# The first block turned tile by tile, block 1's root on ScalarE, and block 1 turned earlier

## What is computed

```python
xn = _layernorm(x, axis=-1)
# branch 1
h = tanh(einsum('btd,ed->bte', xn, W1) + b1)
s = (einsum('btd,od->bto', h, w2) + b2)[..., 0]
e = exp(s - max(s))
ctx = cumsum(e * xn) / cumsum(e)              # along the sequence
attn = tanh(concat(ctx, xn) @ Wc.T + bc)
# branch 2, integer weights scaled by 1/127
ffn = (silu(xn @ wg.T) * (xn @ wu.T)) @ wd.T  # hidden width 768
out = x + attn + ffn
```

## Time and profile before

| what | us |
|---|---|
| median of 3 runs | 393.87 (393.25 to 393.88) |
| the profiled execution | 393.06 |
| its span, first to last instruction | 391.1 |
| TensorE (PE) busy in it | 385.9 |
| VectorE (DVE) busy | 297.5 |
| ScalarE (ACT) busy | 235.6 |
| GpSimd (POOL) busy | 210.1 |

### The profile page before, as it was taken

One profiled execution on the slowest core, in us unless ns is written; L12 is line 12 of the kernel. 1 busy time (PEld: TensorE's weight loads), 2 busy tenths in 40 slices (PEclk: granted clock), 3 DMA queues, 4 the chain that ended last, 5 costly groups with the idle time before them and its releaser, 6 DMA issues.

```text
span 391.1 us, 7885 instructions
## 1 busy us (share of the span) xinstructions
PE 385.9 (99%) x2740; PEld 268.7 (69%) x2740; DVE 297.5 (76%) x632; ACT 235.6 (60%) x434; POOL 210.1 (54%) x289
## 2 busy tenths in 40 slices
PE   8999999999999999999999999999999999999996
PEld 4556676757566686866877676767677676676765
DVE  6799998999996997876769966777676765754351
ACT  4766576689985659786556575364553644536250
POOL 1487586874629989794335405866456554502000
PEclk9999999999999999999999999999999999999999
DMA  8944525576834232475210005043231220100001
GB/s 275 348 158 69 137 53 134 106 189 89 201 72 96 54 83 81 116 165 97 76 34 29 27 28 164 28 128 87 58 72 55 90 85 26 54 28 28 28 28 61
DMA packets 54945, 36.56 MB, mean 93 GB/s; under 512 B 31858, under 2 KB 50292, under 8 KB 54900
## 3 DMA queue, kind: packets, MB, share of 16 engines
q1 hardware_dynamic: 54608, 35.73, 35.5%
q10 hardware_dynamic: 292, 0.26, 0.2%
HBM read 20.19 MB, written 8.45 MB: 73 GB/s over the span
## 4 chain that ended last, share of the span: by engine, by line
PE 97%; DVE 2%; issue 0%; DVEq 0%
PE bank L707 44%; PE bank L743 41%; PE bank L763 9%; PE bank L1381 1%; DVE ex L1121 0%; DVE stats L951 0%; PE bank L700 0%; PE bank L1377 0%; DVE veps L980 0%; DVE xt L1091 0%; DVE bank L1116 0%; DVE sg L1413 0%; PE bank L813 0%; DVE mv L955 0%; PE bank L819 0%
## 5 line engine op out<-in xcount | busy, mean ns | idle before, releaser
L743 PE MATMUL bank<-xt,narrow 128*128 128x512 f16 x768 | 177.3, 379 | 0.0
L743 PEld LDWEIGHTS bank<-xt,narrow 128*128 128x128 f16 x768 | 75.2, 98 | 75.4 <-DVE wide L1121 0.2
L707 PE MATMUL bank<-narrow,wide 128*128 128x256 f16 x792 | 96.4, 273 | 0.0
L707 PE MATMUL bank<-narrow,xt 128*128 128x256 f16 x768 | 92.8, 273 | 0.3 <-DVE xt L1091 0.3
L707 PEld LDWEIGHTS bank<-narrow,xt 128*128 128x128 f16 x768 | 75.0, 98 | 19.0 <-DVE xt L1091 0.6
L1258 POOL TENSOR_TENSOR wide<-ex,wide 128x512 f16<-128x512 f32 x32 | 39.4, 1248 | 87.6 <-ACT wide L909 87.6
L888 ACT ACTIVATE sg<-bank 128x512 f32<-128x512 f32 x96 | 57.2, 596 | 46.3 <-PE bank L743 45.6
L1116 DVE SCALAR_TENSOR_TENSOR bank<-bank,sg 128x512 f32<-128x512 f32 x96 | 66.1, 694 | 24.4 <-PE bank L743 21.3
L707 PEld LDWEIGHTS bank<-narrow,wide 128*128 128x128 f16 x792 | 77.5, 98 | 9.4
L895 ACT ACTIVATE wide<-bank 128x512 f16<-128x512 f32 x90 | 53.3, 596 | 47.7 <-DVE bank L1116 39.3
L1121 DVE TENSOR_TENSOR wide<-bank,wide 128x512 f16<-128x512 f32 x90 | 60.5, 678 | 9.9 <-ACT wide L895 8.6
(11 more groups left out here) (103 smaller groups left out, 262.3 us busy)
## 6 DMA issues: line engine op xcount, KB each, us to landing
rows<-scratch SPq DMA_DIRECT2D x16, 512.0 KB, 5.1
out_y<-xres SPq DMA_DIRECT2D x31, 256.0 KB, 2.1
xres<-in_x SPq DMA_DIRECT2D x15, 512.0 KB, 5.1
xt<-xt SPq DMA_TRANSPOSE x56, 2.5
wide<-in_wg SPq DMA_DIRECT2D x1, 768.0 KB, 5.9
wide<-in_wu SPq DMA_DIRECT2D x1, 768.0 KB, 8.4
wide<-in_wd SPq DMA_DIRECT2D x1, 768.0 KB, 10.1
wide<-in_wc SPq DMA_DIRECT2D x1, 512.0 KB, 11.1
```

Of the source, the lines that this page charges most:

```text
L707: return pe.matmul(dst, lhs, rhs, start=False, stop=stop, skip_group_check=True)
L743: mm = pe.matmul(b[:, :], pg.up(which, k, j), pg.xn(sx, k, tok), start=n == 0, stop=n == len(todo) - 1)
```

## The change

- The first block is turned tile by tile: `turn_tile` (step L0) turns one tile of 128 tokens into its own bank, X0 (ScalarE) and Y0 (VectorE) make its high part and remainder, and `first_scores` takes the tiles as they come: high parts with W1's high part for all four tiles, then with W1's remainder, then the remainders. Normalising signals after each tile.
- The bias of block 0's S isn't seeded by ScalarE: four float32 products of one row (`seed_first`), two for each of the two banks, stand behind the warm-ups, which are 6 and not 12; one pair of fills follows instead of two. Ea and the spreading of b1 and w2 on TensorE go. b1 and w2 come by two broadcasting DMAs on SyncE's queue, b1 between wu and wd, w2 between x of block 2 and wc; ScalarE's Ss waits for the first and VectorE's first Sv for the second.
- ScalarE takes the square root straight from the variance, with eps as the bias; VectorE's step that adds eps is gone. Block 1's root is made in this way too (step Rq, then R by `root_first`), without GpSimd's Newton rounds. The silu table (Tb) is loaded behind it.
- GpSimd converts wg and wu in halves of three groups each. Its normalising keeps x * r + s; its cost in `STEP` is 1.1 instead of 0.75.
- Block 1's turns are placed at 2.0 instead of 2.5. Th of blocks 0 and 1 writes to SBUF (`rows`) and frees its bank; their Sv is due 25 us after S instead of 0.8.

```diff
-    "T": (PO, 1.35, 1.45), "N": (PO, 3.2, 3.3), "Cl": (PO, 1.2, 1.3), "Lp": (PO, 0.75, 0.85), "Xm": (PO, 1.5, 1.6),
+    "T": (PO, 1.35, 1.45), "N": (PO, 3.2, 3.3), "Cl": (PO, 1.2, 1.3), "Lp": (PO, 1.1, 1.2), "Xm": (PO, 1.5, 1.6),
...
-BEGIN = {TE: 7.3, SE: 5.7, VE: 8.1, PO: 1.0, SY: 12.0}
-SENT = {"W1h": 6.0, "Ea": 7.0, "Wgh": 9.4, "Wuh": 12.8,
+BEGIN = {TE: 6.9, SE: 5.7, VE: 7.8, PO: 1.0, SY: 12.0}
+SENT = {"W1h": 6.4, "Wgh": 8.9, "Wuh": 12.5,
         "Wdh": 22.0, "K1": 36.0, "Kc": 38.0, "Wch": 50.0}
-X_SENT = (0.0, 11.1, 20.0)
+X_SENT = (0.0, 10.4, 20.0)
...
-        turn = 2.5 + 3.55 * (i - 1) if i else -2
+        turn = (2.0 if i == 1 else 2.5 + 3.55 * (i - 1)) if i else -2
...
-            due["Th", i, pr], due["Sv", i, pr] = end["S", i, pr] + 0.1, end["S", i, pr] + 0.8
+            due["Th", i, pr], due["Sv", i, pr] = end["S", i, pr] + 0.1, end["S", i, pr] + (25.0 if i < AWAY else 0.8)
...
     if kind == "Tb":
-        return [(("Xh", 0, 1), 0)]
+        return [(("X0", 0, 3), 0), *((("Rq", g, 0), 0) for g in range(1, ROOTS))]
+    if kind == "Rq":
+        return [(("B", i, 1), 0)]
...
+        def turn_tile(pe, t):
+            pe.wait_ge(v_xn, t + 1)
+            for k in range(KD):
+                mm = pe.transpose(bank_of(fits, "L0", 0, t)[:, k * P:(k + 1) * P], xnat[:, t // 2, t % 2, k * P:(k + 1) * P], ident[:, :])
+            mm.then_inc(p_x0, 1)
+
+        def first_scores(pe, pr):
...
+            if not pr:
+                pe.wait_ge(a_w, 1)
+                for t in range(4):
+                    pe.wait_ge(a_x0, t + 1)
+                    onto(t, 0, 0)
+                pe.wait_ge(v_w, 1)
+                for t in range(4):
+                    onto(t, 0, 1)
+            for t in (2 * pr, 2 * pr + 1):
+                pe.wait_ge(v_x0, t + 1)
+                mm = onto(t, 1, 0, True)
+            mm.then_inc(p_s, 1)
...
+        def square_root(act, g):
+            act.wait_ge(v_mv, 2 * g + 2)
+            act.activation(rstd[:, columns(g)], mv[:, columns(g), 1], ACT.Sqrt, bias=eps[:, 0:1]).then_inc(a_root, 1)
...
             elif kind == "Ss":
-                act.wait_ge(a_b, 1)
                 act.wait_ge(p_warm, 1)
+                act.wait_ge(s_b1, 16)
...
-                act.activation(b[:, :], b[:, :], ACT.Tanh, scale=1.0 / pg.sum_up).then_inc(a_s, 1)
+                act.activation(rows[:, i, n, :] if i < AWAY else b[:, :], b[:, :], ACT.Tanh, scale=1.0 / pg.sum_up).then_inc(a_s, 1)
...
             elif kind == "Sv":
                 if (i, n) == (0, 0):
-                    dve.wait_ge(a_b, 1)
+                    dve.wait_ge(s_w2, 16)
...
             sp.dma_start(half(wu32.bitcast(I32)), rows_of(wu)).then_inc(s_wu, 16)
+            sp.dma_start(b1_every, biases[0:D].partition_broadcast(P)).then_inc(s_b1, 16)
             sp.dma_start(wd32.bitcast(I32).rearrange("p (k n) -> p k n", k=KH), rows_of(wd)).then_inc(s_wd, 16)
             load_x(sp, 2)
+            sp.dma_start(w2b, w2b2_in[0:D].partition_broadcast(P)).then_inc(s_w2, 16)
...
-            to_every(bank[BANKS - 1], 0, b_row)
-            to_every(bank[BANKS - 1], D, w2_row).then_inc(p_b, 1)
...
-            for n in range(FILL):
-                warm_up(spare_bank)
+            for n in range(2):
+                seed_first(n)
+
+            for n in range(WARM, WARM + FILL):
+                warm_up(n)
```

## The result

The changed kernel takes 395.99 us in the median of 11 runs (394.35 to 397.4), the kernel before 393.39 us beside it (11 runs, 392.99 to 394.2). The ratio is 1.006, with a 95% interval of 1.0042 to 1.0077: slower by 1.7 to 3.0 us, where 393.5 was forecast with a range up to 395.1. The runs also spread more, over 3.05 us against 1.2. The profiled execution took 395.93 us with a span of 394.1 (before: 391.1).

The account below looks back on a forecast made before the run. PE's back-to-back matmuls were taken as the bound. First S 0.7 earlier, less a 0.9 stall before S(1,0), put the milestone at 26.1 against 26.46: 0.35 gained, so 393.5 us against a median of 393.87, range 392.5 to 395.1.

Parts of the forecast that it names:

- The opening: From warm-ups to PE's first S: first S at 8.56 instead of 9.26, 0.7 us earlier.
- from 5.34 on 0.265: Opening's bias seeds on PE: a record takes 0.53 at half clock, 0.265 from 5.34 us on.
- The third rival: Opening: clock not up in time, seeds, fills and transposes at half clock; +4.5 us, 398; chance 0.05.
- The w2b wait: VectorE: Sv, set ahead of H 0, waits for w2b landing at 16.5; H 0 at 18.05, now 16.35.
- The stall of 0.9: PE before S(1,0): waits for its bias seed, starting at 20.0 against 19.14.
- Block 1: Block 1's statistics, root and normalising: small steps to 13.5, Lp 14 to 16.2, no new wait.
- The silu table: ScalarE's table load behind block 1's root: load 1.28, Sg 0 at 15.0 to 15.6, cost nothing.
- Block 2: VectorE's root for block 2 ends near 26.85, GpSimd's rounds 3.0 us later; no cost taken.
- the second rival: PE near 40 us waits for block 2's last transpose: net +0.9, 394.8, slower; chance 0.15.
- The rest of the span: PE after the milestone: the same matmuls, back to back, so no change in time.
- It does less than it says: Rival: a second small wait behind Hh 0, 0.3 to 0.8; 393.9 to 394.3, no change; chance 0.15.

Follow-up runs that it names:

- e10: Changed kernel with only the planner's cost of Lp (GpSimd's normalising) put back to 0.75 and 0.85: 395.16 us, ratio 1.0047.
- e14: Kernel before with tanh of blocks 0 and 1 in SBUF and wu's conversion started with the first dot product: one run, 394.43 us against 393.25.
- e1: Changed kernel with 12 warm-ups instead of 6: 395.10 us, ratio 1.0053 to the kernel before.
- e2: Changed kernel with w2b's transfer issued right behind b1's, ahead of wd: 395.25 us, ratio 1.0043 to the kernel before.
- e3: Changed kernel with 12 warm-ups and w2b's transfer ahead of wd: 394.01 us, ratio 1.0012 to the kernel before.
- e5: e4 with the planner's cost of Lp put back to 0.75 and 0.85: 392.42 us, ratio 0.9971 to the kernel before.
- e8: Kernel before with 6 warm-ups instead of 12: 394.30 us, ratio 1.0021.
- e4: Changed kernel with bias seeds over 128 rows and w2b's transfer ahead of wd, six warm-ups: 393.23 us, ratio 0.9995 to the kernel before.
- e7: Changed kernel with 128-row seeds, w2b left late, planner told Sv can't start before 17.6: 392.47 us, ratio 0.9974 to the kernel before.
- e9: Kernel before with 6 warm-ups and its two spreading products over 128 rows: 393.03 us, ratio 0.9989.
- e11: Changed kernel with 128-row seeds, Sv planned at w2b's landing and block 1's turns at 2.5: 392.19 us, ratio 0.9970 to the kernel before.
- e12: Kernel before with only tanh of blocks 0 and 1 moved to SBUF: one run, 393.67 us against 393.05.

## Why the prediction was wrong

**The opening: wrong, and the step that failed is the clock.** Six warm-ups end at 4.29 (forecast 4.1) and the seeds start at 4.41 (4.5). But the sum went on with "from 5.34 on 0.265", the rise that the earlier trace rows show behind twelve dense products, as if it came at a time of its own, whatever PE had done before; in the changed kernel's trace it came at 12.10. The seeds end at 8.16 for 7.05, the fills at 9.13 for 7.5, the transposes at 10.83 for 8.56, which is 2.27 late (0.09 of it a slip in the sum: 7.05 and 0.54 make 7.59). The third rival had the mechanism (seeds 8.7, fills 9.6, transposes 11.7) at a chance of 0.05. Its argument against, the granted clock full on the page, is worth nothing: that row also reads full where the spacing is doubled. Its price (+4.5) was too high: a bias record takes 0.47 at half clock, not 0.53, the clock came up in the middle of S, and the rest of the delay lay beside the w2b wait.

**The w2b wait: the mechanism right, two terms mis-sized.** The order (Sv ahead of H 0), the releaser, and the way from H 0 to S(1,0) were as forecast: 1.87 us from H 0 to S(1,0) for 1.95. H 0 was 2.0 late (20.05 for 18.05). Of this 0.8 is the landing, 17.3 for 16.5, and the term that was too small is b1's transfer, priced at 0.36 by its bytes:

```profile
10.00:11.00 1.00, 1.00 (x6) 0.87 (x6) 0.99 (x3) 0.90 (x3) 0.25 (x1) 1.00 1.05 250
11.00:12.00 1.00, 1.00 (x7) 0.70 (x5) 1.00 (x4) 0.25 (x1) 0.03 (x1) 1.00 0.88 138
```

These are two stretches of the changed kernel: us, busy us of PE, PEld, DVE, ACT and POOL, the clock column, the DMA share, and last the GB/s moved, 250 and 138, where the kernel before moves 371 and 355. wu lands at the same time in both (11.9 and 12.0) and wd 2.3 behind what is ahead of it in both, but x of block 2 lands at 17.0 for 15.8: with b1 between them the queue needs 1.2 us more, not 0.36. w2b itself, as many bytes, lands 0.4 behind x, as priced. The issues don't explain it: b1's takes 0.89 us and wd's comes at 5.13 for 4.19, yet in e10 b1's takes 0.50, wd's comes at 4.71, and w2b lands no earlier, at 17.45. Why the rate falls there stays open. The rest of the 2.0 is mainly the dot product: 2.59 from the first to H 0, where four at the durations of the earlier trace rows made 1.49. The forecast left out that the change moves tanh from PSUM to SBUF, and that GpSimd was converting; e14 shows the price.

**The stall of 0.9: not there.** PE came to S(1,0) at 21.91 and its seed was ready at 21.87. Both late paths met within 0.04 us, which is why, by the medians, each single repair (0.85 and 0.7 us in e1 and e2) brings less than its share of the 1.9 that both bring (e3). From S(1,0) to the milestone it took 6.25 for 6.07.

**Block 1: nearly right.** VectorE's five steps end at 14.9 for 13.5, since the second half's statistics start behind the late opening, and Lp runs from 15.08 to 17.26 for 14 to 16.2. In the changed kernel nothing waits for it, because PE is late: with w2b early the dot products meet Lp, stretch it from 2.18 to 3.09, and PE waits 0.98 for it in e2 and 0.6 in e5, in whose profiles the clock was up early (5.03 and 5.50). "No new wait" held only under cover of the other delays. **The silu table** cost nothing, as forecast.

**Block 2: the second rival did not happen.** GpSimd's rounds start at 26.35 for 23.84, 2.5 later for the 3.0 reckoned, and PE has no gap near 40.

**The rest of the span: named, not priced.** "The forecast fails upwards if the replanned order opens gaps beyond 60 us" was right, and cost 0.83 at 108.72. The sum took these 361.29 us as the same matmuls, back to back; they are the same, but for one wait.

**"It does less than it says":** no second wait behind Hh 0 was seen.

Together: 26.1 became 28.17 at the milestone (+2.07), and the order added 0.83. That is the 2.9 us between the gain of 0.35 that was forecast and the loss of 2.6 that was measured.

## What to carry over

Before cutting warm-up products, look at what PE does right behind them, here at how many rows the next products contract, and read the clock from the spacing of like matmuls, over several executions; a column that reads full from the first microsecond proves nothing. A planner that is given a new transfer must be given its landing, and its new order must be searched for waits over the whole span, not near the edit alone. When an operand moves from PSUM to SBUF, look at what GpSimd does beside its readers.

## What the runs showed of the hardware that I had not expected

- Behind six warm-ups, full clock came at 12.10 us (changed kernel), 11.94 (e10), 9.76 (e8) and 5.03 (e2) where one-row products followed, and at 4.63 to 7.45 in all six profiles where they had 128 rows, all but one of them zeros (e4 to e7, e9, e11). The medians follow: 2.0 us from e2 to e4, 1.5 from e8 to e9 against the kernel before. The Trainium skill ("TensorE: Matmul & The Clock Gate", Part 1) has the slow clock as the default and sustained activity as what releases it; the runs agree.
- When the clock rises varies between executions of the same dense opening: behind twelve warm-ups it came at 5.39 in the profile of before and at 6.48 to 7.31 in those of e1, e3 and e12 to e14. The 5.34 on which the sum stood was itself an early one.
- GpSimd's conversion and a dot product from SBUF exclude each other for a whole instruction, at 1.2 us for a step of 0.4.
- A broadcast of 128 KB can cost its queue far more than its bytes: with b1 in it, the queue was 1.2 us later at x of block 2, where 128 KB at the rate of the weights take 0.36; w2b, the same size, took 0.4 in the same trace.
